# Two layers of attention on one core: score banks ranked behind the maxima's for reuse, and the maxima dealt to seven steps

## The reference, cut to what matters

```python
# layer 0, per head: text tokens 0..76, image tokens 77..255
out = softmax(q @ k_text.T / 4) @ v_text + softmax(q @ k_ip.T / 4) @ v_ip
x1 = out @ Wo.T + bo + x
# layer 1, per head: text tokens 0..251, image tokens 252..255
probs_t = softmax(q @ k_t.T / 4)
text_out = probs_t @ v_t
qsem = l2norm(probs_t @ text_ehs)            # 512 long, per row and head
fused = q @ k_ip.T / 4 + 0.5 * qsem @ l2norm(ip_ehs).T
ip_out = (softmax(fused) * spatial_mask) @ v_ip
out = (text_out + ip_out) @ W_out + b_out + x1
```

## Time and profile before

| | |
|---|---|
| three runs | 816.4, 819.1 and 819.14 us, median 819.1 us |
| the profiled execution | 815.98 us, its span 814.2 us |
| PE busy | 741.8 us, 91% of the span |
| DVE, ACT, POOL busy | 567.5, 424.7 and 394.3 us (70%, 52%, 48%) |
| one block of layer 0 (block 4) | about 36.1 us |
| one block of layer 1 (block 12) | about 57.1 us |

### The profile page before, as it was taken

One profiled execution on the slowest core, in us unless ns is written; L12 is line 12 of the kernel. 1 busy time (PEld: TensorE's weight loads), 2 busy tenths in 40 slices (PEclk: granted clock), 3 DMA queues, 4 the chain that ended last, 5 costly groups with the idle time before them and its releaser, 6 DMA issues. The chain is left out here.

```text
span 814.2 us, 17550 instructions
## 1 busy us (share of the span) xinstructions
PE 741.8 (91%) x6422; PEld 574.5 (71%) x6422; DVE 567.5 (70%) x1579; ACT 424.7 (52%) x915; POOL 394.3 (48%) x297
## 2 busy tenths in 40 slices
PE   5889999999999898989998998998998989988896
PEld 4767687877878686767776776766776767656574
DVE  4457566665768576767596697787787886786665
ACT  5235646374555646465465554645654654545551
POOL 5521302020110302024387778678668767778873
PEclk9999999999999999999999999999999999999999
DMA  9977746583756555554083243342432620500010
GB/s 278 231 194 196 192 127 165 168 213 91 197 134 193 143 159 109 182 129 150 13 216 103 82 126 106 106 130 69 129 108 69 145 97 23 143 1 15 21 33 18
DMA packets 104356, 101.90 MB, mean 125 GB/s; under 512 B 10408, under 2 KB 103504, under 8 KB 104272
## 3 DMA queue, kind: packets, MB, share of 16 engines
q1 hardware_dynamic: 103632, 100.46, 44.4%
q10 hardware_dynamic: 640, 0.33, 0.2%
HBM read 61.67 MB, written 36.74 MB: 121 GB/s over the span
## 5 line engine op out<-in xcount | busy, mean ns | idle before, releaser
L1383 POOL TENSOR_TENSOR Y<-P,wkv 128x512 f32<-128x512 f32 x160 | 207.0, 1317 | 126.9 <-ACT P L904 126.9
L541 PE MATMUL pB<-wkv 128*128 128x512 f32 x560 | 155.7, 417 | 21.1 <-ACT P L904 19.0
L541 PEld LDWEIGHTS pB<-wkv 128*128 128x128 f32 x560 | 104.1, 195 | 57.9 <-ACT P L904 29.1
L1145 DVE TENSOR_TENSOR Y<-pB,Y 128x512 f32<-128x512 f32 x160 | 107.5, 688 | 37.2 <-PE pB L541 32.7
L1129 DVE TENSOR_REDUCE m_sb<-pB 128x2 f32<-128x504 f32 x160 | 106.8, 676 | 30.7 <-PE pB L491 30.5
L1359 POOL TENSOR_TENSOR klo<-xin,khi 128x256 fp32r<-128x256 f32 x18 | 13.2, 754 | 223.4 <-ACT khi L809 223.4
L894 ACT ACTIVATE wkv<-pB 128x512 fp32r<-128x512 f32 x160 | 86.5, 593 | 62.7 <-PE pB L526 35.1
L904 ACT ACTIVATE P<-pB 128x512 f32<-128x512 f32 x160 | 86.6, 598 | 48.9 <-PE pB L521 26.1
L904 ACT ACTIVATE P<-pB,ln 128x512 f32<-128x512 f32 x160 | 101.4, 694 | 0.0
L809 ACT ACTIVATE Vs<-pPV 128x512 f32<-128x512 f32 (+1 forms) x80 | 39.2, 490 | 99.4 <-PE pPV L573 59.0
L1127 DVE TENSOR_REDUCE m_sb<-pB 128x2 f32<-128x358 f32 x160 | 83.7, 523 | 0.0
(11 more groups left out here) (161 smaller groups left out, 1283.8 us busy)
## 6 DMA issues: line engine op xcount, KB each, us to landing
QP<-q0d SPq DMA_DIRECT2D x64, 192.0 KB, 4.5
KP<-k0d SPq DMA_DIRECT2D x64, 192.0 KB, 4.7
c_sb<-in_cT SPq DMA_DIRECT2D x16, 512.0 KB, 5.5
q0d<-qhi SPq DMA_DIRECT2D x32, 256.0 KB, 2.8
k0d<-khi SPq DMA_DIRECT2D x32, 256.0 KB, 2.4
q0d<-qlo SPq DMA_DIRECT2D x16, 256.0 KB, 2.8
k0d<-klo SPq DMA_DIRECT2D x16, 256.0 KB, 2.6
VB<-vipd SPq DMA_DIRECT2D x6, 640.0 KB, 4.3
```

The lines of the kernel that those rows point to most:

```text
L541: made = mm(bank[:, :], G[i][:, col:col + 128], ph[:, src, :, :].rearrange("p a s -> p (a s)"), start=(n == 0), stop=(n == len(jobs) - 1))
L1145: tt(y, bank_of["gp", q, dst][:, :], y, MUL).then_inc(dv_y, 1)
L1383: tt(y, w, r.bitcast(F32), SUB).then_inc(po_y, 1)
```

## The change

The third edit stamps the score banks of layer 1's halved steps 3.5 counts later than they are given back; other banks given back up to three counts later are then reused before them. The first edit deals the ten pairs of maxima to seven steps (2, 1, 2, 1, 2, 1, 1) where there were six (2, 1, 2, 0, 2, 1, 2), so step 3 gets one pair and becomes a halved step, step 6 has one pair in place of two, and the last pair is still in step 6. It holds for blocks 0 to 14. The instructions, their sizes and the order of all other items stay.

```diff
-PAIRS = (2, 1, 2, 0, 2, 1, 2, 0, 0, 0)
+PAIRS = (2, 1, 2, 1, 2, 1, 1, 0, 0, 0)
...
-            def give(bank):
+            def give(bank, behind=0):
+
                 clock[0] += 1
-                at[id(bank)] = clock[0]
+                at[id(bank)] = clock[0] + behind
                 del held[id(bank)]
...
                 for bank in banks:
-                    give(bank)
+                    give(bank, 3.5 if halves and u >= B else 0)
```

## The result

The changed kernel takes 793.1 us (median of 4 runs, 790.9 to 796.6) against 817.75 us for the kernel before (4 runs, 812.8 to 819.1). The ratio is 0.9713, 95% interval 0.9656 to 0.977. The profiled execution takes 792.34 us, 23.6 less than the 815.98 of before, with a span of 790.5. (One run among the experiments, at a mean clock of 0.655, took 997.5 us and is left out.)

The account below looks back on a forecast made before the run. PE was taken to bound the kernel, busy for 91% of the span. Layer 1's 22.1 us and layer 0's 6.1 sum to 28.2 off the profiled 815.98, giving 787.8; it predicted 789 us, range 780 to 803.

Parts of the forecast that it names:

- Block 12: Layer 1: waits for exponentials P become waits for each step's first maximum; 2.9 us won, also used for blocks 10 to 13.
- step 5, nothing: Block 12, step 5: the first quad still waits 0.6 us for a normalization, so nothing is won.
- Steps 2 and 3: Block 12: step 2's quads start 1.23 us earlier, step 3 pays 0.28 and waits for Y; 0.76 us won together.
- The other blocks of layer 1: Block 8 wins 2.8 us, block 9 5.5, blocks 10 to 13 2.9 each, block 13 another 1.5, block 14 0.7.
- The clock doesn't follow: Rival, chance 0.08: the two half-clock stretches, in blocks 9 and 13, stay or fall elsewhere; 3 us less won, 792.
- the halved pass at 0.04 us: Step 3's new halved pass costs 0.28 us, step 6 gets 0.24 back; 0.04 us net a block.
- the 0.3 us a block tried with that rule: Step 3's mode-change drain charged again at both ends: 15 × 0.3 = 4.5 us, a sum of 792.
- eight blocks: Layer 0: waits before the shift's transposes go in eight blocks, less 0.04 us each for the halved pass; 6.1 us won.
- DVE takes over: Rival, chance 0.22: DVE's queue grows by 1 us in steps 2 to 6; the kernel wins 17 us, 802.
- Only the pairs matter: Rival, chance 0.08: the quads meet banks no sooner free, and only layer 0's 6 us stay; 811.
- The other side: Rival, chance 0.03: first maximum comes later than first P in steps 0, 2 and 4 of layer 1 blocks; 827.
- a sign of being wrong: L573's waits for Y growing over 1 us a step, or maxima starting over 0.8 us after scores in steps 2, 4, 6.

Follow-up runs that it names:

- rank_only: The changed kernel with the ranking of score banks kept but the old deal of pairs: 802.95 us, ratio 0.9835 to the kernel before.
- pairs_only: The changed kernel with the new deal of pairs kept but the banks ranked as before: 812.1 us, ratio 0.9946 to the kernel before.
- norm2: The changed kernel with DVE's normalization of step 4 put ahead of the low part of K's second projection: 792.9 us (3 runs), ratio 0.9725.
- norm_first: The changed kernel with an edit meant to put the normalization ahead of K's low part on DVE, which moved nothing: 791.3 us, ratio 0.9692.
- first_old: The changed kernel with the old deal of pairs in block 0 alone: 791.9 us, ratio 0.9684 to the kernel before.
- dve_more: The changed kernel with one small maximum, read by nobody, added to each of layer 1's maxima: 799.25 us (one run).
- late3: The changed kernel with step 3's pair of maxima at the step's end and its scores not halved: 799.8 us, ratio 0.9789.

## Why the prediction came out

The sum was 28.2 us against the profiled execution; 23.6 were measured. Its mechanism was right: the order of banks that the two programs fix, played through, is the prediction's table at every step of block 12, and each wait for P turned into the wait, or into none, that the sum had. The missing 4.6 us are two terms of layer 0 (1.1 and 3.1) and the set-up (1.3), less 0.9 that layer 1 won beyond its sum.

- *Block 12.* Predicted by step: 0, -0.23; 1, 0; 2 and 3, +0.76; 4, +0.68; 5, 0; 6, +1.68; 2.9 in all. Measured: -0.23, 0, +0.83, +0.64, -0.31, +1.71; 2.6. The term that failed is "step 5, nothing": PE came earlier, DVE was held inside its subtraction until GpSimd's instruction ended, and the quads wait 0.3 us longer for ST (rank_only, pairs_only; norm2 takes it away).
- *Steps 2 and 3.* The predicted split was 1.23 won, 0.28 paid for the halved pass and 0.19 for a wait for Y. rank_only, with no pair in step 3, wins 1.23 in step 2 (5.61 to 4.38 us from the scores' first weight load to the next). The halved pass and its pair then cost 0.40, not 0.28 (steps 2 and 3 of rank_only beside the changed kernel's), and no wait for Y is left in block 12's step 3. That the sum held is in part luck: two errors of 0.12 and 0.19 cancel.
- *The other blocks of layer 1.* 8: 3.9 us for 2.8; 9: 4.7 for 5.5; 10 to 12: 2.6 each for 2.9; 13: 4.2 for 4.4; 14: 2.2 for 0.7. Together 23.0 for 22.1. This closeness is luck too: blocks 8 and 14 won some 2.6 more than they were given, and about 2.0 of that lies where half-clock stretches of the trace before are absent after, which the prediction did not count (step 0 of block 8, 8.22 to 7.23 us; step 8 of block 14, 7.29 to 6.28).
- *The clock.* "The clock doesn't follow" fell: the stretches behind the earlier trace rows and in block 13 are gone, and were worth 1.6 us each, where 1.5 was said (step 2 of block 9, 8.65 us before and 7.29 in pairs_only, which pays 0.2 there for the halved pass; step 6 of block 13, 7.33 before, where block 12 has 5.77). That they went because the waits went is not shown. pairs_only keeps the wait of the earlier trace rows and has no half-clock stretch behind it:

```profile
434.56 1.46 PEld L542 LDWEIGHTS pB<-wkv 128*128 128x128 f32 x7 [2.85 <-ACT P L905]
```

```profile
434.60:438.00 3.40, 3.40 (x23) 2.93 (x25) 1.68 (x4) 0.49 (x1) 3.06 (x3) 1.00 0.00 0
```

- *The change without the clock.* The profiled executions had mean clocks of 0.983 before and 0.991 after. A straight line of time over clock through 45 runs of the kernel before (beside the experiments; one of 825.6 us left out) gives 812.4 us at 0.991, one through the eight runs of the changed order (changed and norm_first) 791.4. So I estimate the change at 21 us at equal clock, and 2 to 3 of the 23.6 as the clock's.
- *Layer 0, the halved pass at 0.04 us.* This term was mis-sized: it costs 0.2 more (in block 4, S2 to S4 grows by 0.44 and S6 to S7 falls by 0.99: 0.55 won for the 0.76 predicted). Over blocks 2 to 7, 1.1 us were mis-sized. The rule of the Trainium skill weighed in the prediction, TensorEngine Tiling (Array Packing), Key Properties, that a change of mode drains TensorE, points the right way, but that the drain is the cause is not shown. Of the prediction's two prices, the 0.3 us a block tried with that rule was nearer than the 0.04 in the sum.
- *Layer 0, "eight blocks".* Six blocks win. The time that block 0 won became wait for a DMA, with 1.2 us more of it and a half-clock stretch behind: 1.6 us lost for 1.5 counted as won, 3.1 in all (first_old). Against the start of block 0, PE came 0.3 us earlier and the rows 1.0 us later: their transfers start 27.5 us (27.6 after) behind step 0's scores, but PE's wait ends 6.2 us after that start before and 7.0 now. Two weight loads go ahead of them on SP's queue, issued 2.9 us ahead before and 2.3 now, and the wait ends 9.1 and 9.3 us after these, so the loads seem to set it. That is read from the traces, not tested.
- *Set-up*, +1.3 us: a half-clock stretch at 32.8 us that another run of the same order didn't have (norm_first).
- *Rivals.* "DVE takes over" is answered by dve_more: 20 more instructions on DVE, 0.3 us. "Only the pairs matter" had 811 for a change that took 793, and pairs_only, the deal without the ranking, takes 812 us. The other side needed the first maximum to come behind the first P; it decides only in step 0, as the prediction had it.

What it said the profile would show: the waits for P gone, the wait for the first maximum's copy in step 0 (1.03, where 0.8 was said) and step 4 (0.37) hold; so do L504's waits. Block 12 is at 54.4 us for 54.2, block 4 at 35.6 for 35.3. In blocks 10 to 13 the waits for Y grew in step 1 alone, by 0.16. But in step 3 of block 9 a new one of 0.92 us stands, and in step 3 of block 14 one of 2.66, where there was none over 0.3: by over 1 us, which the prediction had named as a sign of being wrong. In block 14 DVE's products did come too late for PE (S3 to S4 grew from 4.96 to 7.13 us), and the block still won 2.2.

## What to carry to other kernels

When a buffer is handed out by when it was given back, rank it by when it comes free, which is when its slowest reader ends; check which engine is the next releaser and price each place by that, since here the two halves of the change were worth 1.55 and 0.15 us a block alone and 2.6 together. When a stall goes, follow the same engine to its next wait: step 5's wait for ST took back 0.3 us of the 2.9 predicted, and one item moved in DVE's queue was then worth 0.8. Time won just ahead of a wait for a DMA is not won, and here the longer wait cost more than was saved. And before a gain is put down to an edit, count the half-clock stretches in both traces.

## What was not expected of the hardware

- The 64x4 subtraction on DVE, with both inputs in SBUF, took 0.39, 0.67, 1.04 or 1.30 us in block 12 and ended 0.01 to 0.03 us behind GpSimd's instruction, but 0.15 us where GpSimd was idle. Its 128x8 sister of K's first projection took 0.17 us in the changed kernel, where GpSimd's instruction ended 0.1 us before it did, 0.48 before and 1.03 in late3, where it ended with GpSimd's again. The profile lists this as busy time of DVE, so a small instruction with a duration that changes from kernel to kernel can be a wait in disguise.
- At the end of block 0, a wait of PEld of 2.3 to 2.7 us was followed by 3.4 us or more at a granted clock of 0.50 in nine traces of nine, one of at most 1.14 us in none of five. The length of the wait alone does not decide: in pairs_only a wait of 2.85 us (434.56) had none behind it, nor had one of 2.66 us in block 14 of the changed kernel.
- The mean granted clock goes with most of the spread between runs of one kernel: 0.975 to 0.994 with 818.9 to 811.0 us.
